# Cross-attention features as three passes of rounded high and low parts, in place of full-precision products

## The chip, the cores and the metric

One core of one Trainium2 chip runs the kernel. The metric is the time of one execution on the device, in microseconds (us). Engines are called PE (TensorE; PEld its weight loads), DVE (VectorE), ACT (ScalarE), POOL (GpSimd) and SP (SyncE, which here only issues transfers).

## The reference, cut to what matters

The program is one layer: cross attention, self attention, mixture of experts. Only the cross attention is touched. For 32 batches of 64 rows (D = 512) and a context of 1601 rows:

```python
Sim = (hc @ w1)[:, :, None] + (ctx @ w2)[:, None, :] + einsum('bid,bjd->bij', hc * w3, ctx) + b_sim
A = softmax(Sim, axis=2)
hq_hat = einsum('bij,bjd->bid', A, ctx)                 # attended rows
hc_bar = einsum('bi,bid->bd', softmax(max(Sim, 2), 1), hc)
feats = concatenate([hc, hq_hat, hc * hq_hat, hc * hc_bar], -1)
x = x + feats @ W_qv + b_qv                             # W_qv is 2048 x 512
```

`W_qv` is four blocks of 512 rows. The two middle ones meet the attended rows (`hq_hat`) and the product rows (`hc * hq_hat`). The first and last are folded together by DVE into one block `Wc` for each batch.

## The kernel before, in words

The rows are 16 tiles of 128 (two batches each). Phase A (cross attention) works on one tile at a time; in stage t, `stage_a(t)`, PE does, in this order: four transposes of the attended rows of tile t-1 (`attended_T`), four of the normed rows of tile t+1 (`normed_T`), `features(t-1)`, a broadcast of the row maxima (`spread_max`), the transposes of the exponentials of tile t (`exp_T`, L1937), `attend(t)` over 13 chunks of the context (L1959) with the four `combined_chunk(t-1)` between them (L1922), and the scores of tile t+1, `similarities(t+1)` (L1862, four chunks k of the inner dimension). A plain float32 matmul of this kernel is two instructions on PE. `features` is eight such matmuls into PSUM bank 5, four with the attended rows `F2` (L1911) and four with the product rows `F3` (L1914).

The other engines go through the same stage by lists of their own. ACT: copies `F2` out of PSUM in two halves (`attended_copy`), the exponential (`exp_scores`, L801), copies of transposes, and the copy `normed_copy`. DVE: row maximum of the scores (`maxima`, L1165 to L1171), `F3 = F1 * F2` (`features`, L1219), `row_dot`, the first `Wc` chunk (`combined`, L1232), `batch_max`, copies, `queries`, `batch_means`, the other `Wc` chunks, `residual_a`, `attended`.

SP issues the context transfers in a fixed order: transposed context `ctxT` of tile t (L434, eight transfers for four chunks k), then plain context `ctxN` of tile t (L445, L448), then the next tile. There is one buffer for each chunk and batch, so `ctxT` chunk k of tile t waits until the scores of tile t-1 have used chunk k, and `ctxN` chunks wait likewise for `attend(t-1)`. Pieces of `x` come between them after tiles 2, 4 and 5. `W_qv` is loaded once, after the first `ctxN`.

Phase B (self attention) begins with `start_b`, where the last tile's `features(15)` stands among projections (`project`, L2031, and `split_rows`, L2021). Phase B already uses high and low parts: a value is rounded to float32r (the high part) by ACT (L869 for weights), DVE takes the difference (the low part, L1351 for weights), and each product is three matmuls, high by high, high by low, low by high, each one instruction. At the very end POOL gathers expert rows with 32 indirect transfers (L781), whose descriptors are kept in a ring in SBUF that the program's constructor sizes.

Of the kernel before, what the change touches and what calls it, by code (L numbers as in the profile page):

```python
# [14 lines left out]
F32 = mybir.dt.float32  # L15
# [7 lines left out]
P = 128  # L23
# [39 lines left out]
def perceiver_layer(nc, x, ctx_n, ctx_t, w1, w23, b_sim, w_qv, b_qv, wq, wk, wv, wm, b_qk, bv, bm,  # L63
# [8 lines left out]
    with ExitStack() as stack:  # L72
# [40 lines left out]
        ARENA = 42528  # L113
        SPLIT = 21 * KD * P * 2
        with nc.sbuf_tensor("arena", [P, ARENA + T * D], F32) as arena:
            pass
# [22 lines left out]
        split = sb("split", [P, ARENA + T * D], F32R)  # L139
        split_ws2 = split[:, WS:WS + 2 * KF * D].rearrange("p (s k n) -> p s k n", s=2, n=D)  # L140
# [20 lines left out]
        def as_split(v):  # L161

            n = v.shape[1] * v.shape[2]
            return split[:, used[0] - n:used[0]].rearrange("p (a b) -> p a b", b=v.shape[2])
# [5 lines left out]
        w_qv_sb = carve(4 * KD, D)  # L170
        expS = carve(J)
        used[0] += -used[0] % 4
        ET = carve(JC, P)
        hc = carve(D)
        weighted = carve(KD, 2, S)
        qT = carve(KD, P)
        hq = carve(D)
        F1 = [carve(KD, P) for _ in range(2)]
        F2 = carve(KD, P)

        F3 = hq.rearrange("p (k n) -> p k n", n=P)
# [77 lines left out]
        low_lo = ARENA + TR * D, 8192 + 9216 - KA * D, used[0]  # L259
        low_w = [split[:, lo:lo + KA * D].rearrange("p (k n) -> p k n", n=D) for lo in low_lo]  # L260
        at(low_lo[0] + KA * D)
        xg = [carve(D), row_b[:, :]]
        at(low_lo[2] + KA * D)
        iT_p = [as_split(carve(KB, P)) for _ in range(2)]
        interT = carve(KD - KB, P)
        assert used[0] <= low_lo[1], used[0]
        at(WS + KD * FS)
        low_w2 = []
        for _ in range(3):
            low_w2.append(as_split(carve(KB, D)))  # L270
# [62 lines left out]
        def h2T_of_pair(p):  # L333
# [5 lines left out]
        x_early, const_in, wqv_in, wqv_ends_in = (sem(n) for n in ("x_early", "const_in", "wqv_in", "wqv_ends_in"))  # L339
# [21 lines left out]
        rs_ready, hq_ready, hqT_done, F2_ready, F3_ready, hbar_ready, wc_ready, wc_used = (  # L361
            sem(n) for n in ("rs_ready", "hq_ready", "hqT_done", "F2_ready", "F3_ready", "hbar_ready", "wc_ready",
                             "wc_used"))
        mxb_done, bmax_ready, nbmax_ready, bexp_ready, brec_ready, weighted_ready, hsum_ready = (
            sem(n) for n in ("mxb_done", "bmax_ready", "nbmax_ready", "bexp_ready", "brec_ready", "weighted_ready",
                             "hsum_ready"))
        feats_done, x1_ready = sem("feats_done"), sem("x1_ready")

        w_hi_ready, w_lo_ready = sem("w_hi_ready"), sem("w_lo_ready")
        h1_ready, xb2_ready, h1T_done, h1hi_ready, h1lo_ready = (  # L370
# [52 lines left out]
        def _(sp):  # L423
# [35 lines left out]
            sp.dma_start(w_qv_sb[:, KD:3 * KD, :], w_qv_v[:, KD:3 * KD, :]).then_inc(wqv_in, 16)  # L459
            sp.dma_start(w_qv_sb[:, 0:KD, :], w_qv_v[:, 0:KD, :]).then_inc(wqv_ends_in, 16)  # L460
            sp.dma_start(w_qv_sb[:, 3 * KD:4 * KD, :], w_qv_v[:, 3 * KD:4 * KD, :]).then_inc(wqv_ends_in, 16)
# [77 lines left out]
            def load_w2(place, lo, hi):  # L539
                n = hi - lo  # L540
                here = slice(place, place + n * KD * D)
                high, whole = (m[:, here].rearrange("p (e k f) -> p e k f", k=KD, f=D) for m in (split, arena))
# [244 lines left out]
        def _(act):  # L787
# [23 lines left out]
            def after_scores(t, i, first=False, more=True):  # L811
# [12 lines left out]
                if first:  # L824
                    sqrt_of_var(2, 2, TW)
# [254 lines left out]
        def _(dve):  # L1080
# [74 lines left out]
            def maxima(t, first):  # L1155
                dve.wait_ge(sim_done, KD * (t + 1))
                if not first:
                    dve.wait_ge(exp_done, t)
                    dve.wait_ge(mxb_done, t)
# [1305 lines left out]
```

## Time and profile before

| what | value |
|---|---|
| median of 3 runs | 1320.67 us (1318.13 to 1321.43) |
| the profiled execution's own time | 1321.82 us |
| its span | 1320.1 us |
| granted TensorE clock, mean | 0.999 |
| PE busy | 1290.9 us (98% of the span) |
| PEld busy | 807.3 us (61%) |
| DVE busy | 728.5 us (55%) |
| ACT busy | 344.0 us (26%) |
| POOL busy | 168.6 us (13%) |

The time is that of the slowest (here the only) core. The span is from the first to the last instruction that the profiler saw; durations are read inside it, and the 1.7 us around it are the same for every reading here. PE is pipelined, so its busy share says only that it always had something under way; whether it waits is read from the chain of waits and from the rows of the timeline.

### The profile page before, as it was taken

The numbers are of one execution on the slowest core, as the hardware profiler recorded it, in microseconds if no ns is written. First come the engines' busy times: TensorE is split into PE (matmuls) and PEld (weight loads), VectorE is DVE, ScalarE is ACT, GpSimd is POOL, SyncE is SP. The second block draws the span as 40 slices with busy tenths as digits, with TensorE's granted clock in tenths as the row PEclk, the third lists the DMA queues.
The fourth block names the chain that finished last, engine by engine and source line by source line (L and its number), as shares of the span: only waits on it lengthen the run. The fifth ranks groups of instructions, "written<-read, shape, count | busy, mean of one in ns | idle before, by whom it ended". The sixth has DMA issues, their size and how long they took to land.

```text
span 1320.1 us, 21266 instructions
## 1 busy us (share of the span) xinstructions
PE 1290.9 (98%) x7443; PEld 807.3 (61%) x7444; DVE 728.5 (55%) x1370; ACT 344.0 (26%) x614; POOL 168.6 (13%) x173
## 2 busy tenths in 40 slices
PE   6999999999999999999999999999998999999998
PEld 3443444444444443357888888898985677777643
DVE  4445455544444444567877888756434445444446
ACT  2211111111111111234444554341212322223200
POOL 1000000000000000003000114503324000000055
PEclk9999999999999999999999999999999999999999
DMA  9999999999999999822477753132679888999897
GB/s 341 411 395 388 390 393 396 396 396 390 389 387 389 390 388 382 310 99 93 153 272 272 287 202 121 42 124 96 254 251 324 275 288 277 305 311 287 285 348 239
DMA packets 122195, 387.30 MB, mean 293 GB/s; under 512 B 12160, under 2 KB 34688, under 8 KB 122016
## 3 DMA queue, kind: packets, MB, share of 16 engines
q1 hardware_dynamic: 117024, 369.87, 76.6%
q0 software_dynamic: 5120, 16.78, 3.5%
q8 instruction: 28, 0.46, 0.2%
q14 instruction: 23, 0.19, 0.0%
HBM read 328.41 MB, written 58.20 MB: 293 GB/s over the span
## 4 chain that ended last, share of the span: by engine, by line
PE 72%; DMA 18%; SPq 4%; DVE 3%; issue 2%; POOL 0%; ACT 0%; ACTq 0%; POOLq 0%
PE ps L1959 14%; PE ps L1862 13%; PE ps L2031 11%; PE ps L2021 10%; DMA arena<-moe_in 8%; DMA row_b<-moe_in 5%; PE ps L1911 4%; PE ps L1922 4%; PE ps L1914 4%; SPq L602 3%; PE ps L1818 2%; PE ps L1937 2%; PE ps L2412 2%; DMA arena<-ctx_n 2%; PE ps L2050 1%
## 5 line engine op out<-in xcount | busy, mean ns | idle before, releaser
L789 ACT ACTIVATE arena<-ps 128x512 f32<-128x512 f32 (+2 forms) x164 | 77.8, 495 | 541.4 <-PE ps L1922 180.2
L1959 PE MATMUL ps<-arena 128*64 128x512 f32 (+1 forms) x832 | 192.3, 594 | 0.0
L1862 PE MATMUL ps<-arena 128*64 128x512 f32 (+1 forms) x1024 | 178.6, 505 | 2.4 <-DMA arena<-ctx_t 1.7
L2031 PE MATMUL ps<-split 128*128 128x256 f32 x1344 | 170.7, 285 | 1.1 <-DVE split L1330 1.1
L2031 PEld LDWEIGHTS ps<-split 128*128 128x128 f32 x1344 | 163.7, 191 | 5.6 <-issue 3.5
L2021 PE MATMUL ps<-split 128*128 128x512 f32 x648 | 157.7, 396 | 1.1 <-DVE arena L1396 1.1
L1862 PEld LDWEIGHTS ps<-arena 128*64 128x64 f32 x1024 | 66.5, 138 | 122.0 <-issue 118.9
L2021 PEld LDWEIGHTS ps<-split 128*128 128x128 f32 x648 | 118.9, 188 | 27.8 <-issue 2.0
L1232 DVE SCALAR_TENSOR_TENSOR arena<-arena,hbar 128x512 f32<-128x512 f32 x128 | 90.5, 749 | 70.4 <-PE ps L1922 68.9
L1959 PEld LDWEIGHTS ps<-arena 128*64 128x64 f32 (+1 forms) x832 | 58.3, 137 | 112.4 <-issue 111.7
L1165 DVE TENSOR_REDUCE small<-ps 128x1 f32<-128x1601 f32 x15 | 27.4, 1825 | 118.8 <-PE ps L1862 118.8
L692 POOL TENSOR_TENSOR arena<-arena,row_b 128x512 f32 (+1 forms) x16 | 20.3, 1271 | 490.1 <-DVE arena L1122 461.6
L2314 PE MATMUL ps<-arena 128*128 x156 | 73.4, 592 | 1.1 <-ACT split L1057 1.0
L1922 PE MATMUL ps<-arena 128*64 128x512 f32 x256 | 66.0, 594 | 0.0
L781 POOL DMA_INDIRECT arena<-moe_out,slot_i x32 | 34.1, 1067 | 234.9 <-DMA moe_out<-arena 225.5
L1911 PE MATMUL ps<-arena 128*128 128x512 f32 x128 | 58.8, 602 | 0.3 <-ACT arena L789 0.3
L1914 PE MATMUL ps<-arena 128*128 128x512 f32 x128 | 57.5, 592 | 0.0
L789 ACT ACTIVATE arena<-arena 32x512 f32<-32x512 f32 x64 | 40.3, 629 | 36.3 <-DVE arena L1345 33.0
L1631 DVE STREAM_TRANSPOSE zero<-arena 128x512 uint32<-128x512 uint32 x20 | 14.2, 712 | 62.7 <-DMA arena<-moe_in 55.4
L1063 ACT ACTIVATE row_a<-ps 128x512 f32<-128x512 f32 x39 | 23.3, 597 | 86.9 <-PE ps L2343 74.2
L1818 PE MATMUL ps<-ident,arena 128*128 128x128 f32 x256 | 37.3, 276 | 8.0 <-DVE arena L1122 6.8
L756 POOL DMA_INDIRECT moe_in<-arena,idx x32 | 33.2, 1037 | 88.3 <-DVE idx L1716 80.3
(223 smaller groups left out, 1786.1 us busy)
## 6 DMA issues: line engine op xcount, KB each, us to landing
arena<-ctx_n SPq DMA_DIRECT2D x128, 768.0 KB, 16.6
arena<-ctx_t SPq DMA_DIRECT2D x122, 800.5 KB, 19.2
split<-parts_low SPq DMA_DIRECT2D x39, 768.0 KB, 7.3
split<-parts_low SPq DMA_DIRECT2D x39, 512.0 KB, 5.0
moe_in<-zero SPq DMA_DIRECT2D x3, 3328.0 KB, 13.5
moe_out<-arena SPq DMA_DIRECT2D x39, 256.0 KB, 4.9
stage_raw<-w1t SPq DMA_DIRECT2D x8, 768.0 KB, 5.5
parts_high<-split SPq DMA_DIRECT2D x8, 768.0 KB, 7.5
```

Source lines behind the costliest of these rows:

```text
L602: sp.dma_start(xg_of(g)[Q * b:Q * (b + 1), :].rearrange("q (a n) -> q a n", a=NQ), moe_in[P * g:P * (g + 1), P * b:P * (b + 1)].rearrange( ...
L789: return nc.scalar.activation(o, i, ACT.Copy)
L1232: v.scalar_tensor_tensor(Wc[:, h, :], w_qv_sb[:, 3 * KD + k, :], hbar[:, i, k, h:h + 1], w_qv_sb[:, k, :], ALU.mult, ALU.add).then_inc(wc_ ...
L1818: last = nc.tensor.transpose(dst[:, P * k:P * (k + 1)], src[:, P * k:P * (k + 1)], ident[:, :])
L1862: last = mm(bank(n)[S * h:S * (h + 1), 0:w], qT[:, k, S * h:S * (h + 1)], ctxT[h][:, k, at_j:at_j + w], start=(k == 0), stop=(k == KD - 1))
L1911: mm(bank(5), F2[:, k, :], w_qv_sb[:, KD + k, :], start=(k == 0), stop=False)
L1914: mm(bank(5), F3[:, k, :], w_qv_sb[:, 2 * KD + k, :], start=False, stop=False)
L1922: last = mm(bank(5)[r, :], F1[i][:, k, r], Wc[:, h, :], start=False, stop=(k == KD - 1))
L1959: last = mm(bank(7)[S * h:S * (h + 1), :], ET[0:w, c, S * h:S * (h + 1)], ctxN[h][0:w, c, :], start=(c == 0), stop=(c == JC - 1))
L2021: last = mm(dst, lhs[a][:, k, :], rhs[b][:, k, :], start=(k + i == 0), stop=(k == n - 1 and i == 2))
L2031: last = mm(dst[:, 2 * P * m:2 * P * (m + 1)], w[a][:, k, c], tokens[b][:, k, :], start=(k + i == 0), stop=(k == KD - 1 and i == 2))
L2314: mm(dst, raw(k), raw_w(k), start=(k == n), stop=False)
```

## The change

The features of attended and product rows are made in three passes, as phase B does it. ACT rounds the attended rows out of PSUM (banks 6 and 7 now, not 5 and 6) into `F2_hi`; DVE multiplies `F3` straight from PSUM, then takes `F2_lo`; ACT rounds `F3` into `F3_hi`; DVE takes `F3_lo`. The two middle blocks of `W_qv` are split once on chip into `w_mid_hi` and `w_mid_lo`, while the first tile is in work. On DVE `maxima` becomes `row_max` and `diagonal`, and `features` now stands ahead of `row_max`, with the low part of the product between the two. PE's wait for the residual of the tile before moves from `attended_T` to `features`. The wait of the three `W_qv` transfers becomes one. In `batch_means` the semaphore of the reciprocal and DVE's wait for it go. Tiles are laid out anew (the parts lie in the memory of `ET`, `weighted` shares that of `hq`), and the descriptor ring of POOL's transfers is set to 4096 bytes of a partition, where the constructor's default of 16384 stood.

```diff
@@ ACT
                 if first:
+                    for j in range(MID):
+                        round_mid(j)
                     sqrt_of_var(2, 2, TW)
...
-                    copy(F2[:, 2 * j:2 * j + 2, :].rearrange("p a b -> p (a b)"), bank(5 + j)[:, 0:2 * P]
-                         ).then_inc(F2_ready, 1)
+                    nc.scalar.activation(F2_hi[:, 2 * j:2 * j + 2, :],
+                                         bank(6 + j)[:, 0:2 * P].rearrange("p (k n) -> p k n", n=P), ACT.Copy
+                                         ).then_inc(F2hi_ready, 1)
+                act.wait_ge(F3_ready, t + 1)
+                nc.scalar.activation(F3_hi, F3, ACT.Copy).then_inc(F3hi_ready, 1)
+
+            def round_mid(j):
+                act.wait_ge(wqv_in, 48)
+                k = slice(KD * j, KD * (j + 1))
+                nc.scalar.activation(w_mid_hi[:, k, :], w_mid[:, k, :], ACT.Copy).then_inc(w_hi_ready, 1)
@@ DVE
             def features(t, i):
                 dve.wait_ge(F1_ready, t + 1)
-                dve.wait_ge(F2_ready, 2 * (t + 1))
-                v.tensor_tensor(F3.rearrange("p a b -> p (a b)"), F1[i].rearrange("p a b -> p (a b)"),
-                                F2.rearrange("p a b -> p (a b)"), ALU.mult).then_inc(F3_ready, 1)
+                dve.wait_ge(F2hi_ready, 2 * (t + 1))
+                attended = ps[:, 6:8, 0:2 * P]
+                v.tensor_tensor(F3.rearrange("p (j k) n -> p j (k n)", j=2), F1[i].rearrange("p (j k) n -> p j (k n)", j=2),
+                                attended, ALU.mult).then_inc(F3_ready, 1)
+                v.tensor_tensor(F2_lo.rearrange("p (j k) n -> p j (k n)", j=2), attended,
+                                F2_hi.rearrange("p (j k) n -> p j (k n)", j=2).bitcast(F32), ALU.subtract
+                                ).then_inc(F2lo_ready, 1)
+
+            def product_low(t):
+                dve.wait_ge(F3hi_ready, t + 1)
+                v.tensor_tensor(F3_lo, F3, F3_hi.bitcast(F32), ALU.subtract).then_inc(F3lo_ready, 1)
+
+            def mid_low(j):
+                dve.wait_ge(w_hi_ready, j + 1)
+                k = slice(KD * j, KD * (j + 1))
+                v.tensor_tensor(w_mid_lo[:, k, :], w_mid[:, k, :], w_mid_hi[:, k, :].bitcast(F32), ALU.subtract
+                                ).then_inc(w_lo_ready, 1)
...
             def stage_a(t, i, second=False, ahead=True):
-                maxima(t, False)
                 features(t - 1, 1 - i)
+                row_max(t, False)
+                product_low(t - 1)
+                diagonal(t, False)
                 row_dot(t + 1)
...
+            for j in range(MID):
+                mid_low(j)
             attended(0, True)
...
                 low_weights(1)
+                product_low(T - 1)
                 queries_b(0, 1, True)
@@ PE
             def features(t, first=False):
-                for k in range(KD):
-                    if k % 2 == 0:
-                        pe.wait_ge(F2_ready, 2 * t + k // 2 + 1)
-                    mm(bank(5), F2[:, k, :], w_qv_sb[:, KD + k, :], start=(k == 0), stop=False)
-                pe.wait_ge(F3_ready, t + 1)
-                for k in range(KD):
-                    mm(bank(5), F3[:, k, :], w_qv_sb[:, 2 * KD + k, :], start=False, stop=False)
+                for k in range(KD):
+                    if k % 2 == 0:
+                        pe.wait_ge(F2hi_ready, 2 * t + k // 2 + 1)
+                    mm(bank(5), F2_hi[:, k, :], w_mid_hi[:, k, :], start=(k == 0), stop=False)
+                for k in range(KD):
+                    mm(bank(5), F2_hi[:, k, :], w_mid_lo[:, k, :], start=False, stop=False)
+                pe.wait_ge(F2lo_ready, t + 1)
+                for k in range(KD):
+                    mm(bank(5), F2_lo[:, k, :], w_mid_hi[:, k, :], start=False, stop=False)
+                pe.wait_ge(F3hi_ready, t + 1)
+                for k in range(KD):
+                    mm(bank(5), F3_hi[:, k, :], w_mid_hi[:, KD + k, :], start=False, stop=False)
+                for k in range(KD):
+                    mm(bank(5), F3_hi[:, k, :], w_mid_lo[:, KD + k, :], start=False, stop=False)
+                pe.wait_ge(F3lo_ready, t + 1)
+                for k in range(KD):
+                    mm(bank(5), F3_lo[:, k, :], w_mid_hi[:, KD + k, :], start=False, stop=False)
@@ constructor
-    nc = bacc.Bacc("TRN2", target_bir_lowering=False, num_devices=1)
+    nc = bacc.Bacc("TRN2", target_bir_lowering=False, num_devices=1, dynamic_dma_scratch_size=4096)
```

## Rows read from the trace of the kernel before

**Rows 1.** The chain that ended last, phase A: start us, us, what.

```profile
228.02 10.79 PE ps L1862 x64
...
239.84 3.52 PE ps L1911 x8
243.36 3.43 PE ps L1914 x8
...
247.01 1.42 PE ps L1937 x13
...
263.18 10.79 PE ps L1862 x64
...
544.40 10.79 PE ps L1862 x64
```

**Rows 2.** Stage windows: us, busy us of each engine, PEclk, DMA share, GB/s.

```profile
228.00:263.00 35.00, 35.00 (x173) 14.35 (x170) 20.16 (x46) 7.37 (x14) 1.27 (x1) 1.00 1.02 396
```

**Rows 3.** The chain in phase B, two bursts of twelve float32r matmuls.

```profile
631.67 2.95 PE ps L2021 x12
...
635.26 2.75 PE ps L2021 x12
```

**Rows 4.** Timeline of stage 1's start, all engines: start us, us, instruction.

```profile
63.05 1.82 DVE L1165 TENSOR_REDUCE small<-ps 128x1 f32<-128x1601 f32 x1 [7.94 <-PE ps L1862]
...
63.40 0.66 ACT L789 ACTIVATE arena<-ps 128x256 f32<-128x256 f32 x2 [8.79 <-PE ps L1842]
...
63.93 3.67 PE L1911 MATMUL ps<-arena 128*128 128x512 f32 x8
...
65.37 1.60 ACT L801 ACTIVATE arena<-ps,small 128x1601 f32<-128x1601 f32 x1
...
65.42 0.69 DVE L1219 TENSOR_TENSOR arena<-arena 128x512 f32<-128x512 f32 x1
```

**Rows 5.** Groups by shape, phase B: count, busy us, mean ns.

```profile
L876 ACT ACTIVATE split<-ps 128x512 fp32r<-128x512 f32 x16 | 8.7, 596 | 26.0 <-PE ps L1818 22.7 <-PE ps L2021 3.4
...
L1330 DVE TENSOR_TENSOR split<-ps,split 128x512 fp32r<-128x512 f32 x30 | 20.1, 688 | 8.1 <-ACT split L884 7.8
```

**Rows 6.** Timeline of `start_b`: start us, us, instruction, idle time before it.

```profile
584.36 5.51 ACT L869 ACTIVATE split<-w_raw 128x2048 fp32r<-128x2048 f32 x3
...
586.30 2.29 DVE L1351 TENSOR_TENSOR split<-w_raw,split 128x2048 fp32r<-128x2048 f32 x1 [1.04 <-ACT split L869]
```

**Rows 7.** Last `W_qv` transfer, then idle time of DVE and ACT after it.

```profile
L461 SPq DMA_DIRECT2D arena<-w_qv x1: 1870/1870/1870, 27.0 to 27.0; - x1
...
DMA to landing us min/median/max: 15.9/15.9/15.9
...
52.26 0.75 DVE L1214 TENSOR_SCALAR arena<-ps,small 128x512 f32<-128x512 f32 x1 [6.87 <-PE ps L1959]
...
53.93 0.20 ACT L793 ACTIVATE var<-var 128x2 f32<-128x2 f32 x1 [10.61 <-DVE var L1107]
```

**Rows 8.** Last `ctxT` transfer of tiles 6, 7, 15: issue time, time to landing.

```profile
L434 SPq DMA_DIRECT2D arena<-ctx_t x1: 1012/1012/1012, 212.6 to 212.6; - x1
DMA to landing us min/median/max: 22.4/22.4/22.4
...
L434 SPq DMA_DIRECT2D arena<-ctx_t x1: 470/470/470, 249.0 to 249.0; - x1
DMA to landing us min/median/max: 20.6/20.6/20.6
...
L434 SPq DMA_DIRECT2D arena<-ctx_t x1: 333/333/333, 520.7 to 520.7; - x1
DMA to landing us min/median/max: 17.3/17.3/17.3
```

**Rows 9.** POOL's gathers at the end: durations, first and last start, landing.

```profile
L781 POOL DMA_INDIRECT arena<-moe_out,slot_i x32: 942/1017/1397, 1264.3 to 1306.9; - x32
...
DMA to landing us min/median/max: 3.5/6.0/7.9
```

More of the change, by code:

```diff
@@ L159, in carve, with as_split @@
             return v
-        def as_split(v):
+        def as_split(v, whole=split):
             n = v.shape[1] * v.shape[2]
-            return split[:, used[0] - n:used[0]].rearrange("p (a b) -> p a b", b=v.shape[2])
+            return whole[:, used[0] - n:used[0]].rearrange("p (a b) -> p a b", b=v.shape[2])
         at(0)
@@ L541, in load_w2 @@
                 here = slice(place, place + n * KD * D)
-                high, whole = (m[:, here].rearrange("p (e k f) -> p e k f", k=KD, f=D) for m in (split, arena))
+                high, whole = (m[:, here].rearrange("p (e k f) -> p e k f", k=KD, f=D) for m in (all_high, arena))
                 sp.dma_start(high[:, :, 0:KB, :].bitcast(F32).rearrange("p e k f -> p e (k f)"),
@@ L1153, in queries, with row_max @@
                                     w23c[:, 0, k:k + 1], ALU.mult, ALU.add).then_inc(qT_ready, 1)
-            def maxima(t, first):
+            def row_max(t, first):
                 dve.wait_ge(sim_done, KD * (t + 1))
@@ L1167, in maxima, with diagonal @@
                 v.tensor_scalar(nsmax, smax, -1.0, None, ALU.mult).then_inc(nmax_ready, 1)
+            def diagonal(t, first):
                 dve.wait_ge(c_ready, t + 1)
+                if not first:
+                    dve.wait_ge(mxb_done, t)
                 v.scalar_tensor_tensor(smx, smax, cdot, bsim[:, :], ALU.add, ALU.add).then_inc(smx_ready, 1)
@@ L1287, in _ @@
             block_maxima(2)
-            maxima(0, True)
+            row_max(0, True)
+            diagonal(0, True)
             row_dot(1)
@@ L1348, in low_weights @@
             def low_weights(i):
-                dve.wait_ge(w_hi_ready, i + 1)
+                dve.wait_ge(w_hi_ready, MID + i + 1)
                 v.tensor_tensor(w_lo[i], w_raw[i][:, :, :], w_hi[i].bitcast(F32), ALU.subtract).then_inc(w_lo_ready, 1)
             variances(2 * T - 2, 0, T - 2)
-            maxima(T - 1, False)
             features(T - 2, 0)
+            row_max(T - 1, False)
+            product_low(T - 2)
+            diagonal(T - 1, False)
             norm_factors(5, 0, T - 2)
@@ L1833, in normed_T, with attended_T @@
                 transposes(bank(4), hc).then_inc(hcT_done, 1)
-            def attended_T(t, first=False):
+            def attended_T(t):
                 pe.wait_ge(hq_ready, t + 1)
-                if not first:
-                    pe.wait_ge(x1_ready, t)
                 pe.wait_ge(bexp_ready, 2 * (t + 1))
```

94 lines of the change are left out of this document (56 added, 38 removed).

## The prediction

> **What bounds the kernel now.** I read the chain of waits first, because the change touches PE's work in phase A and its worth hangs on whether PE sets the pace there. In the chain the pieces of one stage follow each other on PE without a gap: scores, features, transposes of the exponentials, attend, the next scores. The reader should see that two starts of L1862, 228.02 and 263.18, lie 35.16 us apart, and that the features between them are 3.52 + 3.43 = 6.95 us of it [rows 1]. So a microsecond taken from the features is one off the stage, until something else is late.
>
> The second view is the table of stage windows, for what else is full. The 16 DMA engines are busy at a share of 1.02 in the same stretch [rows 2]: PE never waits for a transfer there, yet the transfers have no rest either. So I looked up, third, when the last chunk of `ctxT` lands and when the scores need it. They need the fourth chunk after three quarters of 10.79 us, 8.09 us into L1862 [rows 1]. Tile 6: issued at 212.6, landed 22.4 later at 235.0, needed at 228.02 + 8.09 = 236.1, margin 1.1 us. Tile 7: 249.0 + 20.6 = 269.6 against 271.3, margin 1.7. Tile 15: 520.7 + 17.3 = 538.0 against 552.5, margin 14.5 [rows 1, 8]. From tile 7 to 15 the margin grows by 12.8 us, 1.6 a tile: the transfers keep a pace of 35.16 - 1.6 = 33.56 us a tile by themselves. That PE is the bound holds, but around tile 6 by one microsecond only.
>
> The fourth view is the timeline at a stage's start, for who must be ready when; the rest are durations.
>
> **The features on PE.** Removed: 16 instructions in 6.95 us. Added: 24 float32r matmuls of the same width. The nearest rows are bursts of twelve: 2.95 us after a phase of other work, 2.75 us when the one before is close [rows 3]. The row of 6.95 us contains 0.09 us of start (3.52 against 3.43), so I take 2 x 2.75 + 0.09 = 5.59 us. Gain 1.36 us a tile. Bounds: with the 2.95 bursts 5.90 us, gain 1.05; at half the pitch of a float32 instruction (3.43 / 8 = 0.429, half 0.214) 5.15 us, gain 1.80. The Trainium skill ("TensorE: Matmul & The Clock Gate", on the back-to-back issue gap) gives columns over 2.4 GHz plus about 2.5 ns, some 216 ns for 512 columns. By it the features would be an estimated 5.2 us; the bursts here run at 0.229 us, and I go by them.
>
> **Who feeds those 24 matmuls.** Times relative to the stage of rows 4. ACT's two copies out of PSUM run from 63.40 to 64.06 and PE starts at 63.93 [rows 4]; the new copies have the same shape and place. DVE then multiplies and subtracts, 0.69 us each [rows 5]: `F3` at 64.85, `F2_lo` at 65.55. PE wants `F2_lo` at its ninth matmul, 63.93 + 0.1 + 8 x 0.229 = 65.86: 0.3 us to spare. ACT rounds `F3` in 0.60 us [rows 5], done at 65.45, wanted at the thirteenth, 66.8. `row_max` now starts 2.45 us later than before (65.5, not 63.05) and lasts 1.82 [rows 4]; with the negation it ends at 67.5, `product_low` at 68.2, and `F3_lo` is wanted at the twenty-first, 68.6: 0.4 us. The exponential then runs from 67.55 to 69.15 (1.60, rows 4) and its accumulator read ends at about 69.3; PE, done with the features at 69.55, wants it after `spread_max` at about 69.75: 0.4 us. `diagonal` ends at 68.8, before `spread_max`. So I cost DVE's 1.38 us and ACT's 0.60 us a tile at nothing, hidden under PE; but there are three margins of 0.3 to 0.4 us in a row, and what exceeds them is paid once a tile. Behind `row_max` on DVE stand `row_dot`, the first `Wc` chunk and `batch_max`; DVE is busy 20.16 of 35 us [rows 2], and attend waits for the chunk only 2.7 us after it starts, so nothing more is due there. PSUM banks 6 and 7 are free again when `F2_lo` is taken, long before `spread_max` and attend write them.
>
> **Splitting the weights.** ACT 2 x 1.84 us, DVE 2 x 2.29 us [rows 6], once. They wait for the last `W_qv` transfer, 27.0 + 15.9 = 42.9. ACT sits idle for 10.61 us up to 53.93, DVE for 6.87 us up to 52.26 [rows 7]. ACT is done at 46.7; DVE starts at 45.4 and ends at 50.0. Cost nothing, with 2.2 us of cover left on DVE; without it `attended(0)` would be late.
>
> **The last tile.** In `start_b` ACT's rounding of the self-attention weights starts 0.6 + 1.0 us later, because `attended_copy` now waits for DVE's product first. DVE, which waited 1.04 us there for ACT already [rows 6], gets to `low_weights(1)` 1.6 us later and has `product_low` (0.69) behind it. The first `Wc` chunk is ready some 2.3 us later than before, at 593.0, and PE, finished 1.36 us sooner at 592.3, wants it then. I charge 0.7 us: this tile gives 0.7, not 1.36.
>
> **What transfers allow.** The order of the transfers is unchanged, their bytes too, and the engines are full, so they land when they landed before. PE may be ahead of its old time by no more than the margin. By tile 6 it would have gained 5 x 1.36 = 6.8 us; it may have 1.1. By tile 7, 1.7 (its margin). From there each tile gains 1.36, less than the 1.6 the margin grows by: 1.7 + 8 x 1.36 = 12.6 at tile 15, inside its 14.5. Then features(14) 1.36 and features(15) 0.7: 14.7 us. About 6 us of the gain are lost around tiles 5 to 7 as waits of L1862 for `ctx_t`. Phase B and the rest shift as a whole. The profiled execution took 1321.82 us, so 1307.1; it stands 1.15 us above the median of the runs, so 1306.0.
>
> **Pitch bounds.** Gain 1.05 a tile: 1.7 + 8.4 + 1.05 + 0.4 = 11.6, 1309. Gain 1.80: the margin caps tile 15 at 14.5, plus 1.80 and 1.1, 17.4, 1303.
>
> **Rivals.** (a) *Transfers don't hold PE back.* PE frees buffers sooner, and if SP's waits for PE were what spaced the transfers out, they move with it. Then 15 x 1.36 + 0.7 = 21.1 us, 1299.6. For it: SP waits on buffers in each tile. Against it: the share of 1.02 [rows 2] and twenty microseconds from issue to landing, a queue that never runs dry. 0.14.
>
> (b) *The operands come late.* The margins of 0.3 to 0.4 us fail, by a slower hand-over between ACT and DVE or by a read of PSUM that two engines share. With 1 us of wait a tile the gain is 0.36: 1.7 + 2.9 + 0.4, less the last tile's, about 5 us, 1316. A `row_max` 1.8 us late beyond the margin would make it no change. For it: a chain DVE, ACT, DVE inside 4.3 us. 0.15 for gains of 3 to 9 us, 0.05 for less.
>
> (c) *Slower, by the descriptor ring.* It shrinks to a quarter. The gathers start 42.6 / 31 = 1.37 us apart and land after 6.0 us [rows 9], so 4.4 are under way at once. If the small ring holds fewer, POOL waits. With two at a time a gather takes 3.0 us, 32 of them 96 us in place of 44, and as the mixing is behind them the end moves by about 50 us: 1306 + 52 = 1358. It decides below four gathers. 
>
> **Chances.** Main case 0.59 (1303 to 1310), (a) 0.14, (b) 0.20 in both parts, (c) 0.07. The range 1299 to 1316 takes in (a) and most of (b) and leaves out about 0.15. What a measurement of this kernel can tell from no change is 0.3%, 4 us. Faster by more: 0.59 + 0.14 + 0.14 = 0.87; within it 0.05; slower 0.08, (c) and a bad (b).
>
> **What the profile after would show.** L1911's and L1914's successors: 24 instructions in about 5.6 us. Starts of L1862's successor 33.8 us apart in the last tiles, and more than that around tiles 4 to 7, with PE idle before it and `ctx_t` as the releaser. No idle time of PE ahead of the exponentials' transposes. Gathers still 1.37 us apart. I am wrong if PE waits for DVE or ACT inside the features, or if the starts are 33.8 us apart from the first tile on.

## The result, and the profile after

The changed kernel takes 1302.62 us, the median of 4 runs (1300.60 to 1309.82), beside 1321.05 us for the kernel before on the same chip (4 runs, 1318.13 to 1322.43). The ratio is 0.9873, 95% interval 0.9830 to 0.9916: faster by 11 to 22 us. The forecast was 1306.0, the range 1299 to 1316. A longer comparison of the same kernel (six runs, below) gives 0.9881, interval 0.9850 to 0.9913, or 15.7 us. The predicted gain was 14.7; it lies inside both intervals, a little below both values.

First the page after: the span, the share of each engine, and what the DMA engines moved in 40 slices of the span.

```profile
span 1298.7 us, 21587 instructions
...
PE 1269.0 (98%) x7571; PEld 829.9 (64%) x7572; DVE 750.0 (58%) x1404; ACT 358.1 (28%) x632; POOL 168.8 (13%) x173
...
GB/s 346 410 396 394 391 389 389 393 394 395 392 392 389 391 389 395 381 113 114 201 254 259 299 200 100 70 94 105 251 279 313 272 306 302 311 304 286 273 343 254
```

The chain that ended last, as in [rows 1], shows both parts of the story: PE paces most stages, and a transfer stands in the chain twice. Columns: start us, us, what.

```profile
51.36 10.79 PE ps L1907 x64
...
85.30 10.78 PE ps L1907 x64
97.11 1.02 PE ps L1958 x4
98.13 0.93 PE ps L1962 x4
...
101.86 0.93 PE ps L1975 x4
...
119.18 10.78 PE ps L1907 x64
...
210.30 23.04 DMA arena<-ctx_t
233.38 2.92 PE ps L1907 x16
...
278.10 23.40 DMA arena<-ctx_t
301.54 2.92 PE ps L1907 x16
...
531.01 10.78 PE ps L1907 x64
...
565.81 3.07 PE ps L2092 x24
...
616.18 2.95 PE ps L2082 x12
```

L1907 is what L1862 was. The six bursts of four (L1958 to L1975) are the features: 1.02 + 5 x 0.93 = 5.67 us in place of 6.95 [rows 1]. From 85.30 to 119.18 a stage takes 33.88 us, where it took 35.16. At 210.30 the chain jumps to a `ctx_t` transfer that lands 23 us later, and PE does only its last 16 score matmuls behind it: tile 6 waited for its data. At 278.10 it does so again, for tile 8, whose last chunk came just late enough to make that stage 0.3 us longer. L2092 at 565.81 is the first projection of `start_b` (L2031 before), L2082 at 616.18 the burst that was L2021 at 631.67 [rows 3].

The waits of PE over the whole span confirm who releases it: line, releaser, us in total, times, longest.

```profile
PE ps L1907 <- DMA arena<-ctx_t: 4.7, 5, 1.0
...
PE ps L1958 <- ACT split L847: 0.3, 1, 0.3
```

L1907 waits 4.7 us in all for `ctx_t`. 1.0 of it falls in the very first tile, where the kernel before waited too (1.7 us); the other 3.7 lie in the scores of tile 5 (0.6, before the last chunk) and tile 6 (1.0 before each of the second, third and fourth chunk). The operands that DVE and ACT make anew (`F3_hi`, `F2_lo`, `F3_lo`) cost PE nothing in this list; the 0.3 us for ACT's part of the attended rows stood in the kernel before as well (L1911 for L789, 0.3 us, once).

The windows of the stretch from the scores of tile 1 to the scores of tile 15 say the same in one row (length, then PE, PEld, DVE, ACT and POOL busy, PEclk, DMA share, GB/s), first of the kernel after, then of the one before:

```profile
51.36:531.01 479.65, 475.90 (x2509) 222.69 (x2506) 250.01 (x514) 86.55 (x181) 17.73 (x14) 1.00 1.02 393
```

```profile
52.21:544.40 492.19, 492.19 (x2397) 202.63 (x2394) 235.09 (x486) 77.69 (x167) 17.81 (x14) 1.00 1.01 391
```

It is 12.54 us shorter, and only after the change has PE idle time in it (3.75 us, the 3.7 of the list behind the first tile). The clock is at its upper level, 2.4 GHz, in both (PEclk 1.00), so no part of the difference is clock. A stage without a wait takes 33.9 us, and 14 of them took 474.7 where no chunk was late (the run with fewer bytes, below). This stretch is 4.9 us longer: the stages with late chunks (34.8, 37.6 and 34.2 us, the ones that end with the start of the scores of tiles 6, 7 and 9) lose about 1.2 us more than the idle time that is listed. DVE works 15 us more here, ACT 9 us more, at no cost.

When did the last `ctxT` chunk land? The issue time and the time to landing for tile 6, 7 and 15, as in [rows 8].

```profile
L447 SPq DMA_DIRECT2D arena<-ctx_t x1: 995/995/995, 210.3 to 210.3; - x1
...
DMA to landing us min/median/max: 23.0/23.0/23.0
...
L447 SPq DMA_DIRECT2D arena<-ctx_t x1: 333/333/333, 245.4 to 245.4; - x1
...
DMA to landing us min/median/max: 21.5/21.5/21.5
...
L447 SPq DMA_DIRECT2D arena<-ctx_t x1: 333/333/333, 518.1 to 518.1; - x1
...
DMA to landing us min/median/max: 20.1/20.1/20.1
```

Tile 6 landed at 233.3 (before 235.0), tile 7 at 266.9 (269.6), tile 15 at 538.2 (538.0). PE needs the chunk of tile 15 at 531.01 + 8.09 = 539.1: a margin of 0.9 us where there were 14.5. PE came 13.4 us sooner, the data did not come sooner at all. In a second profile of the changed kernel (below) the same three chunks landed at 235.0, 268.9 and 540.3, so these times move by one to two microseconds between executions.

Where the 14.7 predicted microseconds are, between the same events of both chains:

| stretch | before | after | gain | predicted |
|---|---|---|---|---|
| scores of tile 1 to scores of tile 15 | 492.19 | 479.65 | 12.54 | 12.6 |
| scores of tile 15 to first projection (580.43, 565.81) | 36.03 | 34.80 | 1.23 | 1.36 |
| first projection to the burst of [rows 3] | 51.24 | 50.37 | 0.87 | 0.7 |
| sum | | | 14.6 | 14.7 |

The rest of the 21.4 us between the two spans is in none of these stretches: phase A began 0.85 us earlier, and some 6 us came after the burst of [rows 3], in pieces of 1 to 1.5 us, on work that the diff doesn't touch. Whether they are chance is only partly known. From the scores of tile 15 to POOL's first gather, where the table has 2.1 us of gain, four traces with the code of the kernel before (it and three of its variants below) take 717 to 723 us, six traces of the changed kernel and its variants 712 to 714, but three more variants of it 717 to 719, one of which has less to do there than any. Traces differ in this stretch by more than 2.1 us. The means of the first two groups are about 6 us apart; the roughly 4 us beyond the 2.1 may be the change's or chance, and nothing here decides it.

### The profile page after: what moved, and what is told of

Its sections match the earlier page's. It is cut to its first block, busy times and chain, and to the rows that moved or that the text cites. A ratio compares the mean times of both kernels' runs of the same rounds, so it can differ in the third digit from the quotient of the medians.

```text
span 1298.7 us, 21587 instructions
## 1 busy us (share of the span) xinstructions
PE 1269.0 (98%) x7571; PEld 829.9 (64%) x7572; DVE 750.0 (58%) x1404; ACT 358.1 (28%) x632; POOL 168.8 (13%) x173
## 4 chain that ended last, share of the span: by engine, by line
PE 85%; DMA 7%; SPq 4%; DVE 2%; issue 1%; ACT 0%; POOL 0%; ACTq 0%; POOLq 0%; DVEq 0%
PE ps L2020 12%; PE ps L2092 12%; PE ps L2082 11%; PE ps L1907 10%; PE ps L2375 5%; DMA arena<-ctx_t 4%; PE ps L1983 4%; PE ps L1865 3%; PE ps L2473 2%; PE ps L2465 2%; PE ps L2391 2%; PE ps L2394 2%; PE ps L2397 2%; SPq L447 2%; SPq L458 2%; PE ps L1998 2%
## 5 line engine op out<-in xcount | busy, mean ns | idle before, releaser
L1907 PE MATMUL ps<-arena 128*64 128x512 f32 (+1 forms) x1024 | 179.2, 505 | 5.5 <-DMA arena<-ctx_t 4.7
L2092 PE MATMUL ps<-split 128*128 128x256 f32 x1344 | 170.7, 285 | 1.1 <-DVE split L1374 1.1
L2092 PEld LDWEIGHTS ps<-split 128*128 128x128 f32 x1344 | 163.7, 192 | 5.6 <-issue 3.5
L802 ACT ACTIVATE arena<-ps 128x512 f32<-128x512 f32 (+2 forms) x132 | 67.2, 523 | 337.5 <-PE ps L1983 180.3
L1907 PEld LDWEIGHTS ps<-arena 128*64 128x64 f32 x1024 | 66.0, 138 | 126.3 <-issue 119.1
L2082 PE MATMUL ps<-split 128*128 128x512 f32 x384 | 96.7, 401 | 1.1 <-DVE arena L1442 1.1
L1245 DVE TENSOR_TENSOR F<-arena,ps 128x512 f32<-128x512 f32 x16 | 11.0, 687 | 140.7 <-ACT split L847 140.7
L2082 PEld LDWEIGHTS ps<-split 128*128 128x128 f32 x384 | 69.7, 188 | 17.7 <-issue 2.0
L794 POOL DMA_INDIRECT arena<-moe_out,slot_i x32 | 34.2, 1070 | 231.7 <-DMA moe_out<-arena 222.2
L2082 PE MATMUL ps<-split_ws,split 128*128 128x512 f32 x264 | 61.1, 390 | 0.0
L2082 PEld LDWEIGHTS ps<-split_ws,split 128*128 128x128 f32 x264 | 49.3, 188 | 10.1
L847 ACT ACTIVATE split<-ps 128x256 fp32r<-128x256 f32 x32 | 10.5, 381 | 162.6 <-PE ps L1887 162.6
L1808 DVE COPY arena<-ps 128x512 f32<-128x512 f32 x39 | 27.0, 691 | 40.0 <-PE ps L2384 40.0
L769 POOL DMA_INDIRECT moe_in<-arena,idx x32 | 33.5, 1047 | 88.8 <-DVE idx L1763 81.5
```

The costliest lines, as they stand in the source:

```text
L769: nc.gpsimd.indirect_dma_start(moe_in, bass.IndirectOffsetOnAxis(ap=idx[k][i][:, :], axis=0), hs[i], None).then_inc(scat[i], 16)
L794: nc.gpsimd.indirect_dma_start(y01[k][i], None, moe_out, bass.IndirectOffsetOnAxis(ap=slot_i[k][:, t:t + 1], axis=0)).then_inc(y01_in[i % ...
L802: return nc.scalar.activation(o, i, ACT.Copy)
L1808: v.tensor_copy(yg[i], bank(3)).then_inc(y_ready, 1)
L1907: last = mm(bank(n)[S * h:S * (h + 1), 0:w], qT[:, k, S * h:S * (h + 1)], ctxT[h][:, k, at_j:at_j + w], start=(k == 0), stop=(k == KD - 1))
L2082: last = mm(dst, lhs[a][:, k, :], rhs[b][:, k, :], start=(k + i == 0), stop=(k == n - 1 and i == 2))
```

## The experiments

The theory (A): PE bounds phase A until it meets the transfers, which keep a pace of their own of about 33.5 us a tile; what PE gains in the first tiles is lost as waits around tile 6. Rivals: the transfers don't matter (PE's gain is simply smaller); DVE and ACT hold PE back; the descriptor ring plays a part. Tiles are counted from 0, "period" is the distance of two starts of the scores.

**The ring alone.** The kernel before, with only the diff's smaller ring.

```diff
-nc = bacc.Bacc("TRN2", target_bir_lowering=False, num_devices=1)
+nc = bacc.Bacc("TRN2", target_bir_lowering=False, num_devices=1, dynamic_dma_scratch_size=4096)
```

> The kernel before with one edit, the descriptor ring of POOL's transfers at 4096 bytes. Theory A (the ring never fills): no change, within 0.3%, the 32 gathers start 1.37 us apart and land after 6.0 us in the median. Rival B (the ring holds fewer than the 4.4 gathers under way): slower by up to 50 us, gathers further apart. Rival C (the ring or the place of the tiles gives something, which would explain the 6 us that the changed kernel gained after phase B): faster by 3 to 6 us, with phase A at its old pace of 35.16 us a tile.

Measured: 1320.40 us (12 runs), ratio 0.9998, interval 0.9976 to 1.0020; periods 35.15 us. The ring does nothing. In the profile after, with the small ring, the gathers are as far apart as in [rows 9]; count, durations, first and last start:

```profile
L794 POOL DMA_INDIRECT arena<-moe_out,slot_i x32: 942/946/1465, 1243.8 to 1286.0; - x32
...
DMA to landing us min/median/max: 3.5/5.6/6.9
```

(1286.0 - 1243.8) / 31 = 1.36 us, and the landing is no later. Rival (c) is out.

**The changed kernel again.** No edit.

> The changed kernel, unedited. Theory A (transfers hold PE back from tile 5 on, 15.5 us are gained by the end of phase B, and the 6 us that the first profile gained after it are chance of that execution): the scores of tile 15 start again near 531 us, with PE idle for ctx_t at tiles 5 to 9, and the gain against the kernel before is 14 to 20 us. Rival B (the 6 us are the change's own): the gain at the first gather is again 20 us or more in the profile.

Measured: 1306.34 us (1301.46 to 1318.61), ratio 0.9881 (0.9850 to 0.9913). The stretch from tile 1 to tile 15 took 479.9 us, within 0.3 of the first profile, so the time in phase A repeats. Rival B of this run is not decided: the first gather started at 1245.4, 18.9 us before that of the kernel before, where it asked for 20 or more and the stretches of theory A give 14.6. The profiled execution is its longest, and PE's waits in it name a late end:

```profile
PE ps L2473 <- DVE arena L1840: 12.7, 2, 12.3
```

That wait, between the mixing steps that follow the gathers, came in single executions of both kernels (9.5 us, at the corresponding place, in the kernel before without part of its transfers), so it isn't the change's. DVE was itself held there for 10.5 us, by something that the profile lists as `remote`; its cause is not shown. The median of one short series is uncertain by it.

**The kernel before, with less attend.** Theory A says that it isn't the features that matter but any microsecond of PE. The matmuls of two of thirteen chunks of attend are left out, so the output isn't the reference's.

```diff
+SKIP = (1, 4)
...
-                    for h in range(2):
+                    for h in range(2 if c not in SKIP else 0):
```

> The kernel before with two of the thirteen context chunks left out of attend (chunks 1 and 4), four matmuls or 1.72 us of PE a tile, a saving on PE alone like the change's, of 27.5 us in sixteen tiles. Theory A (transfers hold PE back around tile 6 and later): PE idle for ctx_t at tiles 5 to 8, time 13 to 17 us shorter. Rival B (PE alone sets the pace): 27 us shorter, starts of the scores 33.4 us apart from the first tile on.

Measured: 1304.21 us, ratio 0.9867 (0.9837 to 0.9897), 17.6 us (13 to 17 were expected, 27 by PE alone), where PE had 4 x 0.43 = 1.72 us a tile less to do. The periods are 33.9 us, 1.3 less than before (DVE stands in the chain for the rest), but for two, 34.81 and 37.84, up to the scores of tiles 6 and 7, and the wait is the same one (1.4 of the 5.4 us in the first tile, 4.0 in tiles 5 and 6):

```profile
PE ps L1863 <- DMA arena<-ctx_t: 5.4, 5, 2.0
```

With none of the new instructions, the same dent at the same tile. So the loss lies between PE's pace and the transfers, not in how the features are made.

**The changed kernel, with much less attend.** Four chunks left out (the same edit, `SKIP = (1, 4, 7, 10)`).

> The changed kernel with four of the thirteen context chunks left out of attend (1, 4, 7, 10), 3.44 us of PE a tile, 30.5 us of PE work left in a stage. Theory A (the transfers have a pace of their own of 33.5 to 33.9 us a tile): starts of the scores 33 to 34 us apart, PE idle for ctx_t in every stage, scores of tile 15 at 520 us or later, time at most 12 us below the changed kernel. Rival B (transfers follow PE, since it frees the buffers sooner): starts about 30.5 us apart, time some 50 us shorter.

Measured, one run: 1302.16 us. PE lost 3.44 us of work in each of 16 tiles, 55 us, and the time is that of the changed kernel within what one run can tell; tile 1 to tile 15 took 475.5 us in place of 479.65. It is the plainest proof that a faster PE had almost nothing left to win. From tile 10 on the periods are 33.15 to 33.72 us, 33.4 in the mean, and the waits and the chain show PE waiting:

```profile
PE ps L1908 <- DMA arena<-ctx_t: 35.0, 34, 2.6
```

```profile
514.44 20.14 DMA arena<-ctx_t
...
534.62 2.94 PE ps L1908 x16
```

The last chunk of tile 15 lands at 534.6, against 538.2. The prediction's 33.56 us, read from how a margin grew, is close to the 33.4 of this kernel, in which the transfers limit every stage.

**Fewer bytes.** 1.05 of 13.1 MB a tile aren't loaded (stale rows are attended to), in both kernels.

```diff
+                            m = 1 if q == NP - 2 and not first else n
-                            sp.dma_start(ctxN[h][:, n * q:n * (q + 1), :],
-                                         main[:, n * q:n * (q + 1), :]).then_inc(ctxN_in[q], 16)
+                            sp.dma_start(ctxN[h][:, n * q:n * q + m, :],
+                                         main[:, n * q:n * q + m, :]).then_inc(ctxN_in[q], 16)
```

> The changed kernel with less to transfer: from the second tile on the fourth group of plain context loads one of its three chunks, 1.05 of 13.1 MB a tile left out (the other two chunks keep the first tile's data). PE's work is the same. Theory A (transfers hold PE back): no wait of the scores for ctx_t, starts 33.9 us apart from the first tile to the last, scores of tile 15 near 527 us where they stood at 531, time 4 to 6 us below the changed kernel. Rival B (the waits cost nothing or come from something else): starts of tiles 6 to 8 still 34.4 to 37.8 us apart, no change in time.

> The kernel before with the same 1.05 of 13.1 MB a tile left out of the transfers (two of three chunks of the fourth group of plain context keep the first tile's data). Theory A (PE is the bound of phase A before, so the transfers cost it nothing): no change within 0.3%, starts of the scores 35.15 us apart, the margins of ctx_t at tile 6 near 10 us in place of 1 to 3. Rival B (transfers slow it too): 4 to 6 us shorter, as in the changed kernel.

Measured: the kernel before 1322.85 us, 1.0008 (0.9986 to 1.0029), periods 35.15: it has nothing to gain from lighter transfers. The changed kernel 1297.14 us, 0.9824 (0.9796 to 0.9852), and its stretch from tile 1 to tile 15 has no hole:

```profile
53.12:527.86 474.74, 474.74 (x2508) 222.13 (x2506) 250.04 (x514) 86.54 (x181) 17.73 (x14) 1.00 0.98 374
```

474.74 against 479.65 us: the 4.9 us are what the late `ctx_t` cost, 3.7 as listed waits and 1.2 around them. In this stretch the same relief is worth nothing before and 4.9 us after. In the whole time the ratios put the changed kernel 7.5 us lower (4 to 6 were expected), with intervals that leave room for 4.9.

**Half of the change.** Only the attended rows in three passes; the product rows as before.

```diff
-                pe.wait_ge(F3hi_ready, t + 1)
-                ... (three passes of F3_hi and F3_lo)
+                pe.wait_ge(F3_ready, t + 1)
+                for k in range(KD):
+                    mm(bank(5), F3[:, k, :], w_mid[:, KD + k, :], start=False, stop=False)
```

> Half of the change: attended rows in three passes, product rows as four full-precision matmuls as before (their low and high parts and the low part of their weight block are not made). Theory A (the gain is PE's, 0.63 us a tile, as long as the margin of the transfers lasts): starts of the scores 34.5 us apart, a wait of 1 to 3 us for ctx_t around tile 6, the scores of tile 15 485 us after those of tile 1, time 7 to 10 us below the kernel before, a little more than half of the change. Rival B (the split costs elsewhere, and the halves don't add): stage longer than 34.6 us.

Measured: 1317.64 us (10 runs), ratio 0.9965 (0.9938 to 0.9992), a gain of 1 to 8 us. Periods are 34.54 us, 0.62 less than before, as expected; but one of 37.73 stands before tile 7. Tile 1 to 15 takes 486.8 us, 5.4 less than before, where 14 x 0.62 = 8.7 had come with no hole. The measured gain, 4.6 us by the ratio, is less than the 7 to 10 expected: the hole took 3.2 us, though by tile 6 PE had gained only 5 x 0.62 = 3.1 and had a margin of 1.1. The chain shows why the tile was so late:

```profile
212.60 23.43 DMA arena<-ctx_t
...
236.08 2.92 PE ps L1903 x16
```

The chunk landed at 236.0, a microsecond later than before [rows 8], with phase A begun at the same time; in the changed kernel it came at 233.3, 1.7 sooner, in its second profile at 235.0. So "they land when they landed before" holds around tile 6 to within one or two microseconds, and which way it errs I can't tell beforehand.

**The order on DVE.** `row_max` ahead of `features` in `stage_a`, as it was before the change; nothing else.

```diff
-                features(t - 1, 1 - i)
                 row_max(t, False)
+                features(t - 1, 1 - i)
                 product_low(t - 1)
```

> The changed kernel with DVE's order of before at the start of a stage: row_max ahead of the features. Theory A (operands come in time only because the features stand first): PE waits for F2_lo about 0.4 us a tile, the stage of PE alone grows from 33.9 to 34.3 us; since the transfers hold PE back at tiles 5 to 8 anyway, only part of 16 x 0.4 reaches the end, 2 to 5 us. Rival B (the order doesn't matter): PE's stage stays 33.9 us and no wait for F2_lo.

Measured: 1311.88 us, ratio 0.9921 (0.9900 to 0.9942), about 5 us slower than the changed kernel. The periods are 34.50 us, and the chain of a stage shows DVE in it where there was PE alone:

```profile
86.92 10.81 PE ps L1907 x64
...
97.75 1.84 DVE small L1187
...
99.69 0.69 DVE F L1245
100.37 0.61 DVE split L1247
...
101.03 1.19 PE ps L1965 x4
102.22 0.93 PE ps L1970 x4
```

```profile
PE ps L1965 <- DVE split L1247: 4.7, 14, 0.4
```

PE now waits for `F2_lo` in 14 stages, 0.3 to 0.4 us each, as expected. Scores, `row_max`, the product, `F2_lo`, and only then PE's third burst, begun 101.03 - 97.73 = 3.30 us after the scores, where it was 99.06 - 96.08 = 2.98 in the changed kernel; with the slower burst (1.19 against 0.93) that makes the 0.58 us a stage. In exchange the wait for `ctx_t` behind the first tile falls from 3.7 to 1.0 us, so that the end moves by less than the stages do. With this order rival (b) would have been at work. With the order of the change, the timeline of stage 1 shows the margins:

```profile
62.56 0.66 ACT L847 ACTIVATE split<-ps 128x256 fp32r<-128x256 f32 x2 [8.79 <-PE ps L1887]
...
63.92 0.68 DVE L1247 TENSOR_TENSOR split<-ps,split 128x512 fp32r<-128x512 f32 x1
64.04 0.63 ACT L851 ACTIVATE split<-F 128x512 fp32r<-128x512 f32 x1 [0.82 <-DVE F L1245]
64.52 1.81 DVE L1187 TENSOR_REDUCE small<-ps 128x1 f32<-128x1601 f32 x1
...
65.02 1.09 PE L1965 MATMUL ps<-split 128*128 128x512 f32 x4
...
66.44 0.68 DVE L1253 TENSOR_TENSOR split<-F,split 128x512 fp32r<-128x512 f32 x1
66.56 1.60 ACT L814 ACTIVATE arena<-ps,small 128x1601 f32<-128x1601 f32 x1 [0.58 <-DVE small L1189]
...
67.82 1.10 PE L1975 MATMUL ps<-split 128*128 128x512 f32 x4
...
68.97 1.58 PE L1998 MATMUL ps<-ident,arena 128*128 128x128 f32 x13
```

`F2_lo` (L1247) is done at 64.60, PE's L1965 begins at 65.02: 0.4 us. `F3_lo` (L1253) 67.12 against 67.82: 0.7. The exponentials (L814) 68.16 against 68.97: 0.8.

**The last 65 rows.** The 1601 rows of a batch are 12 chunks of 128 and a rest of 65, loaded by a transfer of its own into 65 partitions. I had seen DMA throughput drop in each tile where this transfer is under way. The window of one stage, first the kernel after, then the one before; 40 slices of GB/s; the DMA engines' busy share is 80% or more in all of them:

```profile
GB/s 415 415 421 407 421 407 439 403 432 418 403 425 410 434 371 323 231 228 225 248 409 406 363 410 425 410 421 407 422 436 414 407 421 421 406 433 423 409 408 422
```

```profile
GB/s 419 412 434 409 424 415 414 408 419 405 426 419 412 415 423 423 415 409 415 430 390 304 214 310 270 334 344 414 352 415 423 408 414 434 412 420 412 419 420 412
```

A dip to between half and four fifths of the rate for 5 to 6 slices of 0.88 us, while the DMA engines count as busy. The packets tell that it is these transfers' time: in the stage from 228 us on of the changed kernel, their 130 packets of 2048 bytes start between 244.9 and 250.4, and packets of 6404 bytes of the other transfers take 484 ns in the worst microsecond between, 247 ns outside. The first edit cuts the 65 rows into 64 and 1, in both kernels. (PE's waits count the added transfers.)

```diff
-                            sp.dma_start(ctxN[h][0:JT, JM, :], one[JM * P:J]).then_inc(ctxN_in[q], 16)
+                            sp.dma_start(ctxN[h][0:JT - 1, JM, :], one[JM * P:J - 1]).then_inc(ctxN_in[q], 16)
+                            sp.dma_start(ctxN[h][JT - 1:JT, JM, :], one[J - 1:J]).then_inc(ctxN_in[q], 16)
```

> The changed kernel with the last 65 context rows of a batch loaded as 64 rows and one row, in two transfers. In the trace of before, while the transfers of 65 rows are under way (2048-byte packets), a packet of 6404 bytes takes up to 480 ns in place of 250 and the rate falls to 230 to 300 GB/s for some 5 us a tile. Theory A (it is the odd count of rows, and transfers are the bound of the changed kernel): the dip goes, a tile's transfers take 1 to 1.5 us less, the scores of tile 15 start near 527 us, 4 us shorter in all. Rival B (the dip comes from two kinds of transfer being under way together, whatever the rows): the dip stays, no change, or up to 2 us more for the two transfers more a tile.

> The same edit in the kernel before, where the margins at tiles 5 to 7 are 1 to 3 us and nothing waits for the transfers in phase A. Theory A (PE is its bound): no change within 0.3%, while the margins of ctx_t grow if the edit helps the transfers. Rival B (transfers bound it too): some microseconds shorter.

Measured: changed kernel 1306.09 us, 0.9888 (0.9869 to 0.9907); the one before 1320.57, 0.9997 (0.9983 to 1.0011). The dip is weaker, not gone (slices down to 229 GB/s), the wait for `ctx_t` behind the first tile 2.3 us in place of 3.7. Tile 1 to tile 15 took 478.05 us, 1.6 less than in the changed kernel, where theory A wanted about 4; the time is the same within what can be told. An odd number of rows isn't the whole cause.

**Without those transfers.** Only the first tile's are made (later tiles attend to its rows there); 0.27 MB, 2% of a tile's bytes, fall away. (PE's wait for them is set to the first tile's.)

```diff
+                    if q == NP - 1 and not first:
+                        continue
```

> The changed kernel, with the last 65 context rows of each batch loaded for the first tile only (0.27 of 13.1 MB a tile left out, 2%). Theory A (these short transfers cost more than their bytes, since the rate falls to 230 to 300 GB/s while they are under way): the dips in the rate go, a tile's transfers take 1.3 us less where the bytes alone would give 0.7, the wait of the scores at tiles 5 to 8 shrinks from 4.9 us to under 2, the scores of tile 15 start 478 us or less after those of tile 1 (479.6 in the changed kernel, 474.8 with the light transfers). Rival B (bytes alone count): the dips stay, the margin of ctx_t grows by 0.7 us a tile more than in the changed kernel.

Measured: 1299.72 us, ratio 0.9839 (0.9822 to 0.9856), and from tile 1 to 15 474.80 us, no wait for `ctx_t`. The dips are gone. The margin of the last chunk grows by 3.1 us a tile from tile 6 to tile 8 (later it stays near 19, where the transfers wait for buffers), so the transfers' pace there is 33.9 - 3.1 = 30.8 us, against 33.4 to 33.9 with them. 2% of the bytes are worth 0.7 us a tile, the transfers cost about 3, more than the 1.3 expected. So the dip is theirs.

**The rest as 128 rows.** The transfer reads 128 rows, into all 128 partitions; the 63 rows beyond the batch (those of the next one) are read by nobody, and the last batch keeps its 65. Everything is computed.

```diff
-                            sp.dma_start(ctxN[h][0:JT, JM, :], one[JM * P:J]).then_inc(ctxN_in[q], 16)
+                            if isinstance(t, int) and 2 * t + h == B - 1:
+                                sp.dma_start(ctxN[h][0:JT, JM, :], one[JM * P:J]).then_inc(ctxN_in[q], 16)
+                                continue
+                            rows_on = ctx_n.rearrange("b j d -> (b j) d")[bass.ds(2 * J * t + J * h + JM * P, P)]
+                            sp.dma_start(ctxN[h][:, JM, :], rows_on).then_inc(ctxN_in[q], 16)
```

(The last pass of the loop is written out, so that the last batch can differ.)

> The changed kernel, complete, with the transfer of the last 65 context rows of a batch made one of 128 rows into all 128 partitions: behind the 65 rows come 63 rows of the next batch, which nothing reads (the very last batch keeps its 65). 0.26 MB a tile more is moved. Without these transfers of 65 rows a tile's transfers kept a pace of 30.8 us where PE needs 33.9. Theory A (they cost 3 us a tile for 0.7 us worth of bytes because they write 65 of 128 partitions): the dips go, 0.52 MB at 393 GB/s add 1.3 us to 30.8, the margin of ctx_t grows by 1.5 to 2 us a tile, no wait of the scores at tiles 5 to 8, scores of tile 15 474.8 us after those of tile 1 (479.6 in the changed kernel), time 4 to 6 us below the changed kernel's. Rival B (it is the mixing of packet sizes, or the packets of 2048 bytes): dips stay or get longer with twice the packets, time the changed kernel's or up to 10 us more.

Measured: 1296.79 us (5 runs, 1296.38 to 1300.28), ratio 0.9823 (0.9806 to 0.9840): faster than both kernels, 23 us below the kernel before. One stage's DMA view, the waits and the windows of this kernel:

```profile
GB/s 421 419 396 416 394 434 411 426 410 417 425 417 417 432 410 417 410 432 410 417 432 406 423 412 415 422 428 400 421 428 393 421 428 428 400 421 428 407 400 410
```

```profile
PE ps L1913 <- DMA arena<-ctx_t: 1.3, 1, 1.3
```

```profile
51.49:526.31 474.82, 474.82 (x2509) 222.09 (x2506) 250.06 (x514) 86.61 (x181) 17.74 (x14) 1.00 1.01 413
```

No dip, 413 in place of 393 GB/s, more bytes moved in less time. It isn't the packets' size: the 256 packets of a tile's two transfers have the same 2048 bytes, and packets of 6404 bytes beside them take 249 to 259 ns (means by the microsecond, the stage from 228 us on). The margin of the last chunk of `ctxT` grows by 1.8 us a tile from tile 9 to tile 14, a pace of 33.9 - 1.8 = 32.1 us: 1.3 more than with no such transfers at all, which is what their 0.52 MB take at 413 GB/s. PE never waits for `ctx_t` after the first tile, and the whole gain arrives, 492.19 - 474.82 = 17.4 us, 1.24 in each of 14 stages. That is 4.8 us less than the changed kernel's stretch; by the ratios the whole time is 7.7 us less, where 4 to 6 were expected.

## Why the prediction was right, point by point

**PE bounds phase A, by one microsecond at tile 6.** Right: [rows 1, 8] had said it, and the pair with fewer bytes (nothing from lighter transfers before the change, 4.9 us behind it) and the run with less attend (17.6 us from lighter PE work) show both halves. The waits came where they were predicted, at tiles 5 and 6, and tile 8 lost a little once more.

**The features, 5.59 us, a gain of 1.36.** They take 5.67 to 5.7, the gain is 35.16 - 33.9 = 1.23 to 1.28 a stage. The pitch is 0.93 / 4 = 0.233 us, where I took 0.229 from the bursts of [rows 3]. The Trainium skill ("TensorE: Matmul & The Clock Gate", on the back-to-back issue gap) would make it 0.216; the trace is 8% above it (the bursts of [rows 3] were 6% above), and 5.2 us didn't come.

**The chain of operands costs nothing.** Right. I had 0.3, 0.4 and 0.4 us of margin; there are 0.4, 0.7 and 0.8. The experiment on DVE's order shows that they are real: with `row_max`, 1.8 us, in front of `features`, 0.6 us a stage are lost.

**The weight split is hidden.** Nothing in the chain or the waits is due to it, and the scores of tile 1, behind `attended(0)`, began at 51.36, where it was 52.21.

**Transfers land when they landed before.** This carries the result, and holds for the last tile (538.2 against 538.0; 540.3 in the second profile). It is off by 1.7 us at tile 6 and 2.7 at tile 7: those transfers did come somewhat sooner (in the second profile by 0.0 and 0.7). So by tile 7 PE had gained 2.9 us, not the 1.7 of the margin. The other term erred the other way: from tile 7 to 15 9.6 us came, not 8 x 1.36 = 10.9, for the gain per tile is 1.22 to 1.28 and tile 8 lost another 0.3. That 2.9 + 9.6 = 12.5 meets the predicted 1.7 + 10.9 = 12.6 is luck; neither term was right to better than 1.2 us. About 6 us were predicted as lost to `ctx_t`; 3.7 were waited behind the first tile, 4.9 with what is lost around the waits.

**The last tile gives 0.7.** It gave 0.87.

**The rivals.** (a), 21.1 us: out, by the 3.7 us of waits at tiles 5 and 6 and the run with four chunks left out. Its premise was true in part: between the scores of tile 1 and of tile 15 SP waited 206 us in the kernel before, and 52 in the changed one, for buffers that PE had to free. PE freed them sooner, and the last chunk of tile 15 landed no sooner. The first profile, 21.4 us shorter in its span, looks like (a) to the microsecond, and whoever had compared only the two times would have taken it so; the stretch table shows that some 6 us of it lie where nothing was changed. That the measured gain (15.7 and 16.8 us by the two ratios) is a little above the 14.7 isn't explained by anything in the prediction. (b): out with this order, real with the other. (c): out, ratio 0.9998.

**Open.** Behind tile 8 the margin of the last chunk stays at 0.3 to 0.9 us, though PE's stages of 33.9 are longer than the pace of the transfers alone in the run with four chunks left out, about 33.4; in the kernel before with two chunks of attend left out, with the same stages, it grows by 0.5 to 0.8 a tile up to tile 14. Nothing I ran tells why; SP's waits for buffers (52 us in the changed kernel, 29 with four chunks left out, 120 in the kernel before with two left out) show that the transfers' pace and PE's are not wholly separate. Open too is why a transfer into 65 or 64 partitions slows its neighbours. The Trainium skill ("DMA: Bandwidth & Descriptors", The descriptor swizzle) says that in a transfer to 128 partitions each engine writes its own port, engines 0 to 7 those of partitions 0 to 63, engines 8 to 15 the others. By it, a transfer of rows 0 to 64 would send nearly everything to one half of the ports, and 128 rows would restore the even spread. The three runs agree with that (65 rows dip, 64 + 1 still dip, 128 don't), but none separates it from another cause tied to the number of rows.

## What to carry to other kernels

When an engine gives time back, look up when each of its inputs lands and what margin it has: the gain ends where the margin does, and the growth of the margin from tile to tile gives an estimate of the transfers' own pace without an experiment (33.2 to 34.0 us by this reading in six kernels with the same bytes, 33.4 measured where only transfers limited). Then compare stretches between the same events, not spans; here two single spans differed by 21.4 us, and the stretches where the change works by 14.6. And a DMA share of 1.0 isn't full speed: look at GB/s in fine slices, for transfers of 2% of the bytes into half of the partitions took 9% of the time.

## What was unexpected of the hardware

A transfer of 65 rows of 2 KB into 65 partitions brings the rate of all 16 DMA engines from about 415 to some 225 to 250 GB/s for about 4 us (the stage shown), while they count as busy; about 3 us a tile in all, against 0.7 by its bytes. As 128 rows, twice the bytes, both transfers of a tile cost 1.3 us, and the whole stretch runs at 413 GB/s instead of 393. A descriptor ring of a quarter of its size (4096 bytes) made no difference to gathers 1.36 us apart. And single executions of either kernel end 8 to 16 us late behind the first gather (63.0, 69.1 and 71.2 us where the others have 55 to 58), for a reason that the profile doesn't show: a single profile can't be read to better than that at its end.
